# Four layers on one core: own instruction orders for the last slots of the token blocks

## The chip, the cores and the metric

The kernel runs on one core of one Trainium2 chip. The metric is the device time of one execution in microseconds (us), lower is better.

## What is computed

Sixteen sequences of 256 tokens of width 128 go through four layers, each followed by a residual and a layer norm:

```python
x = layernorm(x + mamba(x))            # layer a: state space block
x = layernorm(x + expert_attention(x)) # layer b: 8 heads of 64, 8 experts
x = layernorm(x + linear_attention(x)) # layer c: 16 heads, rotary, gelu
x = layernorm(x + soft_experts(x))     # layer d: softmax over batches and over slots
```

In layer b each token and head picks one of 8 value experts and one of 8 output experts by the largest gate; `values = x @ value_expert[sel]`, causal attention, then the sum over heads of `out @ output_expert[sel]`. Layer c computes q and k with gelu, rotates them, builds one k^T v per head, and normalises. A layer norm needs `1 / sqrt(variance + eps)` of each token.

## The kernel before

`token_blocks` does layers a, b and c, one batch (a sequence of 256 tokens, two halves c = 0, 1 of 128) at a time; `soft_experts` does layer d for all batches and can begin only when the last batch's rows are in DRAM (`x3_stored`), since its softmax goes over the batches.

The token blocks are a software pipeline, written out by hand. Each engine has a function `slot(r, u, a, b, o, c, more)`, which issues in a fixed order the steps of four batches: in slot t layer a of batch t, the attention of layer b of batch t-1, its expert mixing (called o) of batch t-2, layer c of batch t-3. At the end the flags a, b, o switch off: slot 16 has attention of batch 15, mixing of 14, layer c of 13; slot 17 has mixing of 15 and layer c of 14; slot 18 has layer c of 15 alone. Batch 14 is called Y and batch 15 Z. Every engine works its queue in order; semaphores say when a step of another engine is done. The order of the steps in `slot` therefore decides who waits.

Steps of layer b, attention: `b_values(b,u,e)` on TensorE multiplies by value expert e; `b_v(b,e)` on VectorE (L1267) keeps the rows that chose it; `b_scores(b,hp)` computes two heads' scores, `b_max` (L1278) their maxima, `b_probs` on ScalarE the exponentials, `b_turn` transposes them, `b_pt` copies them back, `b_pv` multiplies with the values, `b_rgb` spreads the scale factors, `b_ot` (L1297) applies them. The scores, the transposed scores and the even experts' values share one pair of banks, `ps_v[0]`.

Mixing: `b_choice(b,u,c)` spreads each token's choice into bank `ps_m`; `b_mo(b,u,c,e)` on VectorE (L1308) makes the masked operand, a product, in one of MO = 4 buffers; `b_out(b,c,e)` on TensorE (L630) multiplies it with output expert e and adds into `ps_u`, a part of bank pair `ps_v[1]`. There are 16 of each for a batch. `b_start` puts the residual into `ps_u` first and waits until all values of the next batch are selected, because the odd experts' values go through the same bank. `b_oa` copies the sum, `b_oat` (L639) transposes it into `ps_o`, `b_res` and `b_x2` (L333) normalise it, `b_x2t` (L645) transposes it back.

Layer c: `c_qk`, `c_v`, `c_rot`, `c_krt`, `c_kv`, `c_out` on TensorE all use bank `ps_c`, one after another; `c_q`, `c_v`, `c_qr`, `c_kv`, `c_res`, `c_ln`, `c_x3` (L1381) are VectorE's part; `c_x3t` transposes the result and copies it to be stored. The store of a batch (L368, L372) reads the single buffers `x3` and `x3T`, so `c_x3(b)` waits until both stores of every earlier batch have landed (32 of `x3_stored` for each).

The reciprocal root of a norm is `newton` (L59), run by GpSimd on tiles of 128 x 2: 15 small operations, 14 of them each dependent on one before.

```python
def wait(eng, sem, value):
    if not isinstance(value, int) or value > 0:
        eng.wait_ge(sem, value)
```

Of the kernel before, what the change touches and what calls it, by code (L numbers as in the profile page):

```python
# [2309 lines left out]
```

## Time and profile before

| | |
|---|---|
| median of 3 runs | 1631.72 us (1630.33 to 1632.02) |
| the profiled execution | 1630.81 us, span of its instructions 1628.9 us |
| TensorE matmul busy | 1472.9 us, 90% of the span |
| VectorE busy | 1239.2 us, 76% |
| ScalarE, GpSimd busy | 799.8 us and 791.1 us, 49% each |
| mean granted TensorE clock | 0.97 of 2.4 GHz |

Slots 16 to 18 lie between 988 and 1119 us of the span. Busy time is what the profile sees an engine execute; a matmul's end is modelled, so two matmuls in a row overlap in the listing, and the time from start to start is what one costs. A time in square brackets is how long the engine was idle before that row, with the instruction that ended it.

### The profile page before, as it was taken

What the parts mean: (1) busy time and instruction counts of PE and PEld (TensorE: products, weight loads), DVE (VectorE), ACT (ScalarE), POOL (GpSimd) and SP (SyncE); (2) the same over time, 40 slices, a digit from 0 to 9 for tenths busy, and PEclk for the clock granted to TensorE, in tenths of its full rate; (3) what the DMA queues carried; (4) which work ended last, traced back from release to release, by engine and by line L of the source; (5) the groups of instructions that cost most, each with busy time, mean ns of one, the idle gap of its engine ahead of it and who ended that gap; (6) DMA issues with size and microseconds to landing.
All of it is one profiled execution on the core that took longest, in us unless ns stands there. A gap on an engine that the chain in (4) does not pass through costs nothing. (4 is left out here: it accounts for less than half of the span.)

```text
span 1628.9 us, 33875 instructions
## 1 busy us (share of the span) xinstructions
PE 1472.9 (90%) x11136; PEld 1275.7 (78%) x11136; DVE 1239.2 (76%) x2450; ACT 799.8 (49%) x1782; POOL 791.1 (49%) x2004
## 2 busy tenths in 40 slices
PE   5489999999999999999999999763899999869997
PEld 4366777778777878878778877653899999869997
DVE  4477798898898898898898887542888888836764
ACT  2144444444444544544544543301577677657775
POOL 0332253453453453453553462221777777647764
PEclk9998999999999999999999999875999999989999
DMA  6000000000000000000000000004876776877882
GB/s 228 7 7 1 8 1 14 15 1 14 15 1 14 14 1 14 14 1 14 14 1 14 8 1 8 7 7 133 208 191 184 201 199 177 243 256 299 315 315 75
DMA packets 140762, 132.20 MB, mean 81 GB/s; under 512 B 7377, under 2 KB 130513, under 8 KB 134097
## 3 DMA queue, kind: packets, MB, share of 16 engines
q1 hardware_dynamic: 140624, 130.50, 25.4%
q8 instruction: 71, 1.16, 0.3%
q14 instruction: 67, 0.54, 0.1%
HBM read 73.85 MB, written 56.62 MB: 80 GB/s over the span
## 5 line engine op out<-in xcount | busy, mean ns | idle before, releaser
L630 PE MATMUL bk<-ve_f,oe 128*128 128x128 f32 x2048 | 277.3, 281 | 3.3 <-DVE ve_f L1308 3.3
L630 PEld LDWEIGHTS bk<-ve_f,oe 128*128 128x128 f32 x2048 | 249.4, 193 | 29.4 <-issue 21.9
L1308 DVE SCALAR_TENSOR_TENSOR ve_f<-ps_m,oT 128x512 f32<-128x512 f32 x256 | 172.5, 682 | 5.6 <-PE bk L630 3.5
L2198 POOL TENSOR_TENSOR d_s<-d_ex 128x1024 f32<-128x1024 f32 x32 | 131.8, 4118 | 86.4 <-ACT d_ex L1998 86.4
L1267 DVE COPY_PREDICATED vals<-oh,bk 128x512 f32<-128x512 int32 x224 | 150.5, 725 | 10.1 <-PE bk L398 9.4
L1948 PE MATMUL d_sl<-d_ex,e_prT 128*128 128x128 f32 x1024 | 136.2, 277 | 8.9 <-POOL d_ex L2215 8.9
L1882 PE MATMUL d_lg<-d_phf,d_xtf 128*128 (+1 forms) x1024 | 125.7, 283 | 14.4 <-DMA d_xtf<-x_T 6.8
L1882 PEld LDWEIGHTS d_lg<-d_phf,d_xtf 128*128 128x128 f32 x1024 | 122.7, 200 | 15.2 <-issue 7.2
L1948 PEld LDWEIGHTS d_sl<-d_ex,e_prT 128*128 128x128 f32 x1024 | 125.5, 194 | 9.1 <-POOL d_ex L2215 9.1
L1892 PE MATMUL d_sl<-d_ex,d_xs 128*128 128x128 f32 x1024 | 121.4, 277 | 5.1 <-DVE d_ex L2113 5.1
L977 ACT ACTIVATE ve_f<-bk,r 128x128 f32<-128x128 f32 x128 | 47.3, 370 | 158.5 <-DVE r L1281 158.3
L396 PE MATMUL bk<-veH,x1H 128*128 128x512 f32 x256 | 116.3, 454 | 7.3 <-DVE vals L1267 7.2
L1892 PEld LDWEIGHTS d_sl<-d_ex,d_xs 128*128 128x128 f32 x1024 | 118.5, 194 | 5.5 <-DVE d_ex L2113 5.5
L2095 DVE TENSOR_REDUCE d_nm<-d_lg 128x128 f32<-128x2048 f32 x32 | 73.3, 2291 | 48.2 <-PE d_lg L1882 46.1
L63 POOL TENSOR_SCALAR lnB_v<-lnB_mv 128x2 f32<-128x2 f32 x16 | 3.1, 192 | 213.6 <-DVE lnB_mv L322 213.6
L879 ACT ACTIVATE pt<-bk 128x384 f32<-128x384 f32 x128 | 61.7, 499 | 90.2 <-PE bk L568 89.1
L398 PE MATMUL bk<-veH,x1L 128*128 128x512 f32 x256 | 101.1, 395 | 0.0
L397 PE MATMUL bk<-veL,x1H 128*128 128x512 f32 x256 | 101.1, 395 | 0.0
L2050 ACT ACTIVATE e_prT<-d_lg 128x512 f32<-128x512 f32 x128 | 72.5, 595 | 47.6 <-PE d_lg L1935 47.5
L2215 POOL TENSOR_TENSOR d_ex<-d_ex,e_bias 128x1024 f32<-128x1024 f32 x32 | 74.8, 2366 | 40.0 <-DMA d_ex<-y_slots 39.9
L1142 DVE SCALAR_TENSOR_TENSOR cacc<-cin,cw,cacc 128x256 f32<-128x256 f32 x192 | 86.6, 495 | 3.0 <-ACT cin L879 3.0
L1993 ACT ACTIVATE d_raw<-d_lg 128x512 f32<-128x512 f32 x128 | 71.5, 601 | 32.4 <-PE d_lg L1882 16.5
(285 smaller groups left out, 3748.1 us busy)
## 6 DMA issues: line engine op xcount, KB each, us to landing
logits<-d_raw SPq DMA_DIRECT2D x128, 256.0 KB, 3.4
e_lt<-logits SPq DMA_DIRECT2D x32, 1024.0 KB, 5.9
y_slots<-d_ys SPq DMA_DIRECT2D x64, 256.0 KB, 4.2
d_ex<-y_slots SPq DMA_DIRECT2D x16, 1024.0 KB, 7.6
d_w<-W SPq DMA_DIRECT2D x16, 256.0 KB, 3.4
oe<-xT SPq DMA_DIRECT2D x1, 2048.0 KB, 7.9
xt_in<-xT SPq DMA_DIRECT2D x16, 128.0 KB, 2.3
x_in<-x SPq DMA_DIRECT2D x16, 128.0 KB, 2.4
```

The costliest lines, as they stand in the source:

```text
L396: pe.matmul(ps, lh, rh, start=first, stop=False, skip_group_check=True)
L397: pe.matmul(ps, lh, rl, start=False, stop=False, skip_group_check=True)
L398: return pe.matmul(ps, ll, rh, start=False, stop=last, skip_group_check=True)
L630: last = pe.matmul(ps_u[:, cols], oe[:, hp, e, :], mo[:, n % MO, hp, :], start=False, stop=(e == NE - 1 and hp == HP - 1), skip_group_chec ...
L1142: V.scalar_tensor_tensor(cacc[:, ch, :], cin[:, ch, tap:tap + L], cw[:, ch, tap:tap + 1], cacc[:, ch, :], ALU.mult, ALU.add).then_inc(q["a ...
L1267: ins = V.copy_predicated(vals[:, c, :, :], oh[:, c, :, e:e + 1].bitcast(I32).to_broadcast([P, HB, DH]), ps_v[e % 2][:, c, :].rearrange("p ...
L1308: V.scalar_tensor_tensor(mo[:, n % MO, :, :].rearrange("p a n -> p (a n)"), ps_m[:], float(NE - e), oT[:, u, c, :, :].rearrange("p a n -> ...
L1882: last = pe.matmul(lg[:, k, i, :], xtf[:, b, c, :], phf[:, cols], start=(i == 0), stop=(i == BB - 1), skip_group_check=True)
L1892: last = pe.matmul(sl[:, k, i, :], xs[:, (BK * i + k) * C + c, :], ex[:, u, c, k, i, :], start=(c == 0 and i == 0), stop=(c == C - 1), ski ...
L1948: last = pe.matmul(po[:, c, :], prT[:, c, s, :], yb[:, v, s, :], start=(s == 0), stop=(s == SB - 1), skip_group_check=True)
L2198: G.tensor_tensor(s8[:], part[:, 0:8, :], part[:, 8:16, :], ALU.add).then_inc(n, 1)
L2215: G.tensor_tensor(yb[:, v, rows, :], yb[:, v, rows, :], bias[:, rows, :], ALU.add).then_inc(e["y"], 1)
```

## The change

Slots 16, 17 and 18 are no longer calls of `slot`; each engine has one written list of the steps of all three. `b_start(Y)` and the `b_out(Y)` now stand among the values of Z, `b_choice(Z,1,0)` and `b_oat(Y)` before the end of Z's attention, and layer c of Y among the `b_out(Z)`. Four helper functions choose the bank: the sum and the transposed rows of Y go to `ps_a` (layer a's, free by then), the second choice and layer c of Z to the two halves of `ps_v[0]`. The last batch's three roots (`lnB`, `lnC`, `lnD`) are issued on VectorE with the same `newton`. All other lines of the diff (some two hundred, of which one is shown) write `wait(eng, ...)` as `eng.wait_ge(...)` where the value is positive.

```diff
+Y, Z = NB - 2, NB - 1
+
+def sum_of(b):
+    return ps_a[:, 0:L] if b == Y else ps_u
+
+def rows_of(b):
+    return ps_a[:, L:2 * L] if b == Y else ps_o[:, L:2 * L]
+
+def chosen_of(b, c):
+    return bank[0][:, 1, :] if (b, c) == (Z, 1) else ps_m[:]
+
+def linear_of(b):
+    return bank[0][:, 0, :] if b == Z else ps_c
...
-        wait(sp, q["c_x3"], b + 1)
+        sp.wait_ge(q["c_x3"], b + 1)
...
+        if (b, c) != (Z, 1):
+            wait(pe, q["b_mo"], OUTS * b + NE * c)
+        else:
+            wait(pe, q["b_pt"], HB * NB)
...
     def b_start(b, u):
 
-        wait(pe, q["b_v"], (NE - 1) * capped(b + 2))
-        pe.matmul(ps_u, id_r[:], x1H[:, u, :], start=True, stop=False, skip_group_check=True)
-        pe.matmul(ps_u, id_r[:], x1L[:, u, :], start=False, stop=False,
+        if b == Y:
+            wait(pe, q["a_x1h"], NB)
+            wait(pe, q["a_x1l"], NB)
+        else:
+            wait(pe, q["b_v"], (NE - 1) * capped(b + 2))
+        pe.matmul(sum_of(b), id_r[:], x1H[:, u, :], start=True, stop=False, skip_group_check=True)
+        pe.matmul(sum_of(b), id_r[:], x1L[:, u, :], start=False, stop=False,
                   skip_group_check=True).then_inc(q["b_start"], 1)
...
     def b_oat(b):
-        wait(pe, q["b_oa"], b + 1)
-        wait(pe, q["b_ot"], HP * capped(b + 2))
-        wait(pe, q["b_eg"], capped(b + 3))
+        pe.wait_ge(q["b_oa"], b + 1)
+        if b != Y:
+            pe.wait_ge(q["b_ot"], HP * capped(b + 2))
+            pe.wait_ge(q["b_eg"], capped(b + 3))
         for c in range(C):
-            last = pe.transpose(ps_o[:, L + c * P:L + (c + 1) * P], oa[:, c * P:(c + 1) * P], id_f[:])
+            last = pe.transpose(rows_of(b)[:, c * P:(c + 1) * P], oa[:, c * P:(c + 1) * P], id_f[:])
         last.then_inc(q["b_oat_ps"], 1)
...
     def c_qk(b, u):
-        wait(pe, q["b_x2t"], b + 1)
-        wait(pe, q["c_x3t"], b)
+        pe.wait_ge(q["b_x2t"], b + 1)
+        if b == Z:
+            wait(pe, q["b_pt"], HB * NB)
+        else:
...
-    slot(NB // 2, 0, False, True, True, True, False)
-    slot(NB // 2, 1, False, False, True, True, False)
-    slot(NB // 2 + 1, 0, False, False, False, True, False)
+    b_choice(Y, 0, 0)
+    b_qk(Z, 1, 0)
+    b_gates(Z, 1)
+    b_oat(Y - 1)
+    b_qk(Z, 1, 1)
+    b_qk(Z, 1, 2)
+    b_qk(Z, 1, 3)
+    b_start(Y, 0)
+    b_values(Z, 1, 0)
+    b_out(Y, 0, 0)
+    b_values(Z, 1, 1)
+    b_out(Y, 0, 1)
+    b_values(Z, 1, 2)
+    b_values(Z, 1, 3)
+    b_x2t(Y - 1, 1)
+    b_out(Y, 0, 2)
+    b_values(Z, 1, 4)
+    b_values(Z, 1, 5)
+    c_qk(Y - 1, 1)
+    b_out(Y, 0, 3)
+    b_values(Z, 1, 6)
+    b_values(Z, 1, 7)
+    c_v(Y - 1, 1)
+    b_scores(Z, 0)
+    c_rot(Y - 1)
+    b_out(Y, 0, 4)
+    b_oht(Z)
+    c_krt(Y - 1)
+    b_out(Y, 0, 5)
+    c_kv(Y - 1)
+    b_turn(Z, 0)
+    c_out(Y - 1)
+    b_out(Y, 0, 6)
+    b_turn(Z, 1)
+    b_scores(Z, 1)
+    b_out(Y, 0, 7)
+    b_choice(Y, 0, 1)
+    b_rgb(Z, 0)
+    b_pv(Z, 0)
+    b_out(Y, 1, 0)
+    b_turn(Z, 2)
+    b_turn(Z, 3)
+    b_out(Y, 1, 1)
+    b_scores(Z, 2)
+    b_out(Y, 1, 2)
+    b_pv(Z, 1)
+    b_out(Y, 1, 3)
+    b_turn(Z, 4)
+    b_out(Y, 1, 4)
+    b_rgb(Z, 1)
+    b_turn(Z, 5)
+    b_out(Y, 1, 5)
+    b_scores(Z, 3)
+    b_out(Y, 1, 6)
+    b_pv(Z, 2)
+    b_rgb(Z, 2)
+    b_out(Y, 1, 7)
+    b_choice(Z, 1, 0)
+    c_x3t(Y - 1)
+    b_turn(Z, 6)
+    b_turn(Z, 7)
+    b_oat(Y)
+    b_rgb(Z, 3)
+    b_pv(Z, 3)
+    b_choice(Z, 1, 1)
+    b_start(Z, 1)
+    b_out(Z, 0, 0)
+    b_x2t(Y, 0)
+    b_out(Z, 0, 1)
+    b_out(Z, 0, 2)
+    c_qk(Y, 0)
+    b_out(Z, 0, 3)
+    b_out(Z, 0, 4)
+    c_v(Y, 0)
+    b_out(Z, 0, 5)
+    c_rot(Y)
+    b_out(Z, 0, 6)
+    b_out(Z, 0, 7)
+    c_krt(Y)
+    b_out(Z, 1, 0)
+    c_kv(Y)
+    b_out(Z, 1, 1)
+    b_out(Z, 1, 2)
+    c_out(Y)
+    b_out(Z, 1, 3)
+    b_out(Z, 1, 4)
+    b_out(Z, 1, 5)
+    b_out(Z, 1, 6)
+    b_out(Z, 1, 7)
+    b_oat(Z)
+    b_x2t(Z, 1)
+    c_qk(Z, 1)
+    c_v(Z, 1)
+    c_rot(Z)
+    c_krt(Z)
+    c_kv(Z)
+    c_out(Z)
+    c_x3t(Y)
+    c_x3t(Z)
...
+    b_eg(Z)
+    b_qk(Z, 0)
+    b_qk(Z, 1)
+    b_qk(Z, 2)
+    b_qk(Z, 3)
+    b_v0(Z)
+    b_x2t(Y - 1, 1)
+    c_gelu(Y - 1)
+    b_probs(Z, 0)
+    c_kr(Y - 1)
+    b_probs(Z, 1)
+    b_oht(Z, 1)
+    b_pt(Z, 0)
+    b_pt(Z, 1)
+    b_probs(Z, 2)
+    b_rgb(Z, 0)
+    b_probs(Z, 3)
+    b_pt(Z, 2)
+    b_pt(Z, 3)
+    b_probs(Z, 4)
+    b_probs(Z, 5)
+    b_pt(Z, 4)
+    b_pt(Z, 5)
+    b_rgb(Z, 1)
+    b_probs(Z, 6)
+    b_probs(Z, 7)
+    b_rgb(Z, 2)
+    c_x3t(Y - 1)
+    b_pt(Z, 6)
+    b_pt(Z, 7)
+    b_oa(Y)
+    b_rgb(Z, 3)
+    b_x2t(Y, 0)
+    c_gelu(Y)
+    c_kr(Y)
+    b_oa(Z)
+    b_x2t(Z, 1)
+    c_gelu(Z)
+    c_kr(Z)
+    c_x3t(Y)
+    c_x3t(Z)
...
+    b_gate(Z)
+    b_res(Y - 1)
+    b_mo(Y, 0, 0, 0)
+    b_mo(Y, 0, 0, 1)
+    b_v(Z, 1)
+    b_v(Z, 2)
+    b_x2(Y - 1, 1)
+    b_v(Z, 3)
+    b_mo(Y, 0, 0, 2)
+    b_v(Z, 4)
+    b_v(Z, 5)
+    b_mo(Y, 0, 0, 3)
+    b_v(Z, 6)
+    c_q(Y - 1)
+    b_v(Z, 7)
+    c_v(Y - 1)
+    b_max(Z, 0)
+    c_qr(Y - 1)
+    b_mo(Y, 0, 0, 4)
+    b_mo(Y, 0, 0, 5)
+    c_kv(Y - 1)
+    b_rg(Z, 0)
+    b_mo(Y, 0, 0, 6)
+    c_res(Y - 1, 1)
+    b_mo(Y, 0, 0, 7)
+    b_max(Z, 1)
+    b_mo(Y, 0, 1, 0)
+    b_mo(Y, 0, 1, 1)
+    b_ot(Z, 1, 0)
+    b_mo(Y, 0, 1, 2)
+    b_max(Z, 2)
+    b_rg(Z, 1)
+    c_ln(Y - 1)
+    b_mo(Y, 0, 1, 3)
+    b_mo(Y, 0, 1, 4)
+    b_ot(Z, 1, 1)
+    b_mo(Y, 0, 1, 5)
+    b_max(Z, 3)
+    b_rg(Z, 2)
+    b_mo(Y, 0, 1, 6)
+    c_x3(Y - 1)
+    b_mo(Y, 0, 1, 7)
+    b_ot(Z, 1, 2)
+    b_rg(Z, 3)
+    b_res(Y)
+    b_ot(Z, 1, 3)
+    b_mo(Z, 1, 0, 0)
+    b_x2(Y, 0)
+    b_mo(Z, 1, 0, 1)
+    b_mo(Z, 1, 0, 2)
+    b_mo(Z, 1, 0, 3)
+    b_mo(Z, 1, 0, 4)
+    c_q(Y)
+    c_v(Y)
+    b_mo(Z, 1, 0, 5)
+    b_mo(Z, 1, 0, 6)
+    c_qr(Y)
+    b_mo(Z, 1, 0, 7)
+    b_mo(Z, 1, 1, 0)
+    c_kv(Y)
+    b_mo(Z, 1, 1, 1)
+    b_mo(Z, 1, 1, 2)
+    b_mo(Z, 1, 1, 3)
+    c_res(Y, 0)
+    b_mo(Z, 1, 1, 4)
+    b_mo(Z, 1, 1, 5)
+    b_mo(Z, 1, 1, 6)
+    b_mo(Z, 1, 1, 7)
+    b_res(Z)
+    rsqrt(dve, "lnB", Z, 1.0, EPS, norms["lnB"]["moments"], 2 * C)
+    b_x2(Z, 1)
+    c_ln(Y)
+    c_q(Z)
+    c_v(Z)
+    c_qr(Z)
+    c_kv(Z)
+    c_res(Z, 1)
+    rsqrt(dve, "lnC", Z, 1.0, 1e-12, norms["lnC"]["moments"], 2 * C)
+    c_x3(Y)
+    c_ln(Z)
+    rsqrt(dve, "lnD", Z, 1.0, EPS, norms["lnD"]["moments"], 2 * C)
+    c_x3(Z)
...
+    rsqrt(pool, "lnB", Y - 1, 1.0, EPS, norms["lnB"]["moments"], 2 * C)
+    c_km(Y - 1)
+    c_turn(Y - 1)
+    b_vg(Z)
+    rsqrt(pool, "lnC", Y - 1, 1.0, 1e-12, norms["lnC"]["moments"], 2 * C)
+    rsqrt(pool, "lnD", Y - 1, 1.0, EPS, norms["lnD"]["moments"], 2 * C)
+    rsqrt(pool, "lnB", Y, 1.0, EPS, norms["lnB"]["moments"], 2 * C)
+    c_km(Y)
+    c_turn(Y)
+    rsqrt(pool, "lnC", Y, 1.0, 1e-12, norms["lnC"]["moments"], 2 * C)
+    rsqrt(pool, "lnD", Y, 1.0, EPS, norms["lnD"]["moments"], 2 * C)
+    c_km(Z)
+    c_turn(Z)
```

The lists shown are TensorE's, ScalarE's, VectorE's and GpSimd's, in this order; each takes the place of the same three calls of `slot`.

## Rows read from the trace of the kernel before

**Rows 1.** Stretches A, B, C and the hand-over: start:end, length, busy, clock, DMA.

```profile
987.99:1042.15 54.16, 50.48 (x379) 40.68 (x378) 37.80 (x87) 20.66 (x60) 12.84 (x50) 1.00 0.02 6
1042.15:1083.32 41.17, 26.52 (x168) 22.29 (x169) 19.50 (x47) 3.80 (x9) 10.94 (x48) 0.83 0.02 7
1083.32:1118.24 34.92, 10.27 (x28) 6.09 (x28) 8.71 (x29) 1.92 (x6) 10.93 (x48) 0.53 0.01 4
1118.24:1126.37 8.13, 0.69 (x3) 0.32 (x3) 0.60 (x2) 0.38 (x1) 0.00 (x0) 0.50 0.38 115
```

**Rows 2.** TensorE's timeline in A: start, length, line, tiles, idle before.

```profile
992.79 0.40 PE L396 MATMUL bk<-veH,x1H 128*128 128x512 f32 x1
...
994.19 0.39 PE L396 MATMUL bk<-veH,x1H 128*128 128x512 f32 x1
...
1009.99 1.10 PE L668 MATMUL ps_c<-ql,rot_s 128*128 128x512 f32 x2
1010.92 1.05 PE L630 MATMUL bk<-ve_f,oe 128*128 128x128 f32 x8
1011.81 0.27 PE L540 MATMUL ps_o<-id_f,oh 128*128 128x128 f32 x1
...
1024.29 0.38 PE L552 MATMUL bk<-negb,id_b 128*128 128x256 bf16 x2
...
1025.45 1.16 PE L630 MATMUL bk<-ve_f,oe 128*128 128x128 f32 x8
1026.54 0.65 PE L582 MATMUL ps_o<-pt,vals 128*64 128x256 f32 x4
```

**Rows 3.** VectorE's timeline in A.

```profile
999.41 1.33 DVE L1267 COPY_PREDICATED vals<-oh,bk 128x512 f32<-128x512 int32 x2
1000.63 0.68 DVE L1308 SCALAR_TENSOR_TENSOR ve_f<-ps_m,oT 128x512 f32<-128x512 f32 x1
...
1015.24 0.17 DVE L1289 RECIPROCAL rg<-rs 128x4 f32<-128x4 f32 x1
1015.44 0.17 DVE L1291 TENSOR_TENSOR rg<-rg,gx 128x4 f32<-128x4 f32 x1
...
1025.57 0.96 DVE L1278 TENSOR_REDUCE r<-bk 128x6 f32<-128x768 f32 x1 [0.39 <-PE bk L560]
...
1029.17 0.66 DVE L1308 SCALAR_TENSOR_TENSOR ve_f<-ps_m,oT 128x512 f32<-128x512 f32 x1
```

**Rows 4.** TensorE's timeline in B.

```profile
1043.19 0.41 PE L639 MATMUL ps_o<-id_f,oa 128*128 128x128 f32 x2 [0.71 <-issue]
1049.84 0.69 PE L645 MATMUL ps_o<-id_f,x 128*128 128x128 f32 x2 [6.24 <-DVE x L333]
...
1057.76 1.13 PE L630 MATMUL bk<-ve_f,oe 128*128 128x128 f32 x8
...
1078.05 1.80 PE L630 MATMUL bk<-ve_f,oe 128*128 128x128 f32 x8 [2.32 <-DVE ve_f L1308]
...
1080.08 2.77 PE L630 MATMUL bk<-ve_f,oe 128*128 128x128 f32 x16
```

**Rows 5.** TensorE on tile ps_c, a batch earlier: start:end, length, busy, clock.

```profile
948.00:961.00 13.00, 4.78 (x24) 1.00 0.00 1
```

**Rows 6.** VectorE's timeline in B and C.

```profile
1062.89 0.19 DVE L1352 TENSOR_SCALAR zd<-ps_c 128x32 f32<-128x32 f32 x1 [1.16 <-PE ps_c L690]
...
1065.42 1.28 DVE L1308 SCALAR_TENSOR_TENSOR ve_f<-ps_m,oT 128x512 f32<-128x512 f32 x2
...
1089.22 0.73 DVE L333 TENSOR_SCALAR x<-ps_o,lnB_mv,lnB_y 128x128 f32<-128x128 f32 x2 [4.63 <-POOL lnB_y L76]
...
1111.28 0.60 DVE L333 TENSOR_SCALAR ncn<-rc,lnC_mv,lnC_y 128x128 f32<-128x128 f32 x2 [4.33 <-POOL lnC_y L76]
...
1118.24 0.60 DVE L1381 TENSOR_SCALAR x<-n,lnD_mv,lnD_y 128x128 f32<-128x128 f32 x2 [4.64 <-POOL lnD_y L76]
```

**Rows 7.** Waits of the DMA queue at the end of C: total, times, longest.

```profile
SPq L106 <- DMA x_T<-x3T: 1.4, 1, 1.4
```

More of the change, by code:

```diff
@@ L370, in store @@
                 sp.wait_ge(x_all_in, 32)
-                wait(sp, q["c_x3t"], b + 1)
+                sp.wait_ge(q["c_x3t"], b + 1)
                 sp.dma_start(x3T_dram[:, bass.ds(b * L, L)], x3T[:]).then_inc(x3_stored, 16)
@@ L627, in b_out @@
                 cols = slice(c * P, (c + 1) * P)
-                wait(pe, q["b_mo"], OUTS * b + n + 1)
+                pe.wait_ge(q["b_mo"], OUTS * b + n + 1)
                 for hp in range(HP):
-                    last = pe.matmul(ps_u[:, cols], oe[:, hp, e, :], mo[:, n % MO, hp, :], start=False,
+                    last = pe.matmul(sum_of(b)[:, cols], oe[:, hp, e, :], mo[:, n % MO, hp, :], start=False,
                                      stop=(e == NE - 1 and hp == HP - 1), skip_group_check=True)
@@ L694, in c_x3t @@
             def c_x3t(b):
-                wait(pe, q["c_x3"], b + 1)
+                pe.wait_ge(q["c_x3"], b + 1)
                 for c in range(C):
-                    last = pe.transpose(ps_c[:, c * P:(c + 1) * P], x3[:, c, :], id_f[:])
+                    last = pe.transpose(linear_of(b)[:, c * P:(c + 1) * P], x3[:, c, :], id_f[:])
                 last.then_inc(q["c_x3t_ps"], 1)
@@ L882, in a_cin @@
             def a_cin(b, half):
-                wait(act, q["a_xbc_ps"], 2 * b + half + 1)
+                act.wait_ge(q["a_xbc_ps"], 2 * b + half + 1)
                 wait(act, q["a_conv"], NCH * (TAPS - 1) * b)
@@ L970, in b_probs @@
                 hp, s, a = h // 2, h // 2 % 2, h % 2
-                wait(act, q["b_max"], 2 * HP * b + 2 * hp + 2)
+                act.wait_ge(q["b_max"], 2 * HP * b + 2 * hp + 2)
                 if h >= 4:
@@ L1132, in a_conv @@
             def a_conv(b, half, taps=range(1, TAPS)):
-                wait(dve, q["a_cin"], 2 * b + half + 1)
+                dve.wait_ge(q["a_cin"], 2 * b + half + 1)
                 n0 = (TAPS - 1) * (NCH * b + 2 * half)
@@ L1293, in b_ot @@
             def b_ot(b, u, hp):
-                wait(dve, q["b_rgb"], HP * b + hp + 1)
+                dve.wait_ge(q["b_rgb"], HP * b + hp + 1)
                 wait(dve, q["b_mo"], OUTS * (b - 1))
@@ L1611, in b_vg @@
             def b_vg(b):
-                wait(pool, q["b_v"], (NE - 1) * (b + 1))
+                pool.wait_ge(q["b_v"], (NE - 1) * (b + 1))
                 for c in range(C):
@@ L1625, in c_turn @@
             def c_turn(b):
-                wait(pool, q["c_q"], b + 1)
+                pool.wait_ge(q["c_q"], b + 1)
                 wait(pool, q["c_qr"], 2 * b)
@@ L1802, in store @@
                 sp.wait_ge(ready, READY)
-                wait(sp, e["rows"], C * (b + 1))
+                sp.wait_ge(e["rows"], C * (b + 1))
                 sp.dma_start(out[bass.ds(b * L, L), :].rearrange("(c p) d -> p c d", p=P), xo[:, u, :, :]
```

329 lines of the change are left out of this document (160 added, 169 removed).

## The prediction

> **What bounds the kernel now.** I read the stretches first [rows 1]. The work around the change is three stretches at the end of the token blocks. In the first (987.99 to 1042.15 us, call it A: experts' mixing of batch Y, attention of batch Z) TensorE is busy 50.5 of 54.2 us at full clock, so it sets the pace. In the second (to 1083.32, B: mixing of Z, linear attention of Y) it is busy 26.5 of 41.2 us. In the third (to 1118.24, C: linear attention of Z alone) 10.3 of 34.9 us: there nothing is loaded and one chain of dependent steps sets the time. The soft experts can't begin before the last store, and nothing in them changes, so what A, B and C gain or lose is what the program gains or loses. The timelines of TensorE and VectorE in these stretches [rows 2 to 6] say what each chain is made of.
>
> **What changes nothing.** Most of the diff's lines write the helper `wait` out as `wait_ge`. The helper only leaves out waits on zero or less; all those rewritten are positive. The instructions are the same, cost 0, wherever they stand. The banks of the last two batches take no instruction either; they only permit orders.
>
> **A, the cost.** Work first: the instructions are those of before plus `b_choice(Z,1,0)` and `b_oat(Y)`, together 0.6 us of TensorE. Then waits. Before, TensorE stood idle 3.7 us of A [rows 1]. VectorE had made up to four products `b_mo` before TensorE wanted the first, because `b_start` and all `b_out` stood behind the values and the first scores. In the new order each `b_out(Y,c,e)` stands on TensorE almost directly behind the place where VectorE makes its product, and TensorE takes its queue in order, so whatever VectorE does first is waited for by the values and scores queued behind. I walk both queues with these units: one expert's values 1.40 us, one `b_out` 0.89 to 1.09, one `b_scores` 1.16, the rotation 0.93 [rows 2]; one `b_v` 1.22, one `b_mo` 0.68 when awaited, and from the start of a `b_max` through `b_rg` and `c_ln` to the end of the next product 4.26 [rows 3]; 0.1 to 0.2 from TensorE's last issue to a reader, 0.05 back.
> - `b_out(Y,0,2)` stands before `b_values(Z,4)`; its product stands behind `b_v` 2, `b_x2` and `b_v` 3. `b_v` 2 can start when values 2 are there, 6.2 us into the values (three blocks of values, two of products), so the product is ready 3.8 us later; from 0.2 before until then TensorE has only values 3 and a transpose to do, 1.6: it waits 2.4.
> - `b_out(Y,0,3)` stands before values 6, its product behind `b_v` 5: 1.5.
> - `b_out(Y,0,4)` stands behind the rotation, its product behind `c_qr`, two 512-wide operations like the product itself: 0.2 + 1.4 + 0.7, and 0.3 to 0.7 for `b_max` before them: 2.9.
> - `b_out(Y,1,3)`: product behind `b_max(Z,2)`, `b_rg`, `c_ln`: 0.2 + 4.3, with a `b_out` and a `b_pv` (1.7) to do meanwhile: 2.9.
> - `b_out(Y,1,5)`: product behind `b_ot(1)`, which needs `b_rgb(1)` on ScalarE, queued behind `b_pt` 5: 2.2.
> - `b_out(Y,1,6)` directly behind `b_scores(Z,3)`: product behind `b_max(3)`, `b_rg`: 2.3.
> - `b_oat(Y)` waits for ScalarE's last `b_pt` and `b_oa`: 1.4. Nine small ones (gates, turns, rotation, `c_out`) 2.6.
>
> That is 18.2; each wait is seen about 0.12 shorter because the modelled end of a matmul covers its start, 1.9 over the sixteen, so 16.3 against 3.7. A grows by 12.6 + 0.6, of which I take 12.9 since the long `b_max` is uncertain. Bounds: 0.6 if TensorE never waits more than before, and 15 if each small wait doubles.
>
> **B, the gain.** Before, `b_oat(Y)` starts 1.0 after A and `b_x2t(Y)` 6.65 later; the first `b_out` of Z comes only at 1057.76, behind three linear steps of Y at half clock [rows 4]. New: `b_oat(Y)` is in A, 1.5 before its end, so `b_x2t(Y)` stands 5.1 after A's end; VectorE waits in `b_x2(Y)` for GpSimd's root with the products of Z queued behind, so only `b_out(Z,0,0)` is done by then. From `b_x2t` on: 15 `b_out` at 0.93 are 14.0, six linear steps 3.7 (their rows come to 4.8 with the modelled ends, some 0.17 each [rows 5]), `b_x2t` 0.2. Waits: first product 0.4, `b_out(Z,0,5)` behind `c_v` 1.3, `b_out(Z,0,7)` behind `c_qr` 1.4, `b_out(Z,1,1)` behind `c_kv` 1.1, `b_out(Z,1,4)` behind `c_res` (2.5 from its first operation to the next product [rows 6]) 2.6, `b_oa` 0.6: 7.4. So B is 5.1 + 25.3 = 30.4 against 41.2: minus 10.8. Bounds: minus 18 without these waits, minus 7 if they come to half as much again.
>
> **C, the gain.** VectorE waits three times for GpSimd's roots: 4.63, 4.33, 4.64 us [rows 6]. The root has 15 operations, of which 14 hang on each other. VectorE's own small dependent operations start 0.20 apart, 0.17 long [rows 3]: 14 of them 2.8, and 0.2 for the two that don't wait and for handing over: 3.0. No row shows a root on VectorE; below, 14 at 0.16 are 2.3, above, GpSimd's 4.6 with nothing gained. I take 3.0, nearest to the same operations on the same engine. Gain 1.6 for the first. For the second 1.3 less (`xc`, hidden before by the wait, is now ahead of the root, 0.35), and `c_x3(Y)` (0.5) stands before `c_ln(Z)`: 0.8. For the third 1.6. Sum minus 4.0, bounds 0.5 more and minus 6. `c_ln(Y)` (2.2) is put between `b_x2(Z)` and `c_q(Z)`, where VectorE waits 4.3 for TensorE and ScalarE: hidden; without that cover it would cost 2.2. A wait is added: `c_x3(Z)` needs both stores of Y, and these are now late, because TensorE's `c_x3t(Y)` stands behind `c_out(Z)`. From `c_x3(Y)` to the landed store: transposes 0.7, copy 0.4, handovers 0.2, and some 1.9 to landing (the queue waited 1.4 for the last such store after issuing it [rows 7]): 3.2. `c_ln(Z)` and its root take 2.2 + 3.0: 2.0 to spare, cost 0.
>
> The Trainium skill ("VectorE: DVE Perf Modes", section on the TRN2 errata) gives a fixed cost of about 150 cycles at 0.96 GHz for each VectorE operation, by which a root would be some 2.4 us, an estimate, and C would gain 1.8 more; the trace's 0.20 between starts is what I use.
>
> **The clock.** After 2.3 us of idle at 1078 the granted clock fell from 2.4 to 1.2 GHz: eight matmuls of a `b_out` took 1.80 us, the next sixteen 2.77 [rows 4], against 0.89 and 1.8: with a transpose about 2.0 lost. A now has five waits of 2.2 to 2.9. Where TensorE is slow before a wait that VectorE sets, the wait swallows part of it. I take a third of one such spell, plus 0.7; bounds 0 and four spells, plus 8.
>
> **Sum.** 12.9 - 10.8 - 4.0 + 0.7 = -1.2. The profiled execution took 1630.81 us (span 1628.9 and 1.9 around it), 0.9 under the median, which is inside the runs' spread, so the difference is applied to the median: 1631.7 - 1.2 = 1630.5. Of the full gain of B some nine tenths is paid in A.
>
> **Rivals.**
> 1. Products in time. If VectorE is ahead of the walk in A (the `b_out` set among the values fill holes that VectorE left TensorE there), then half of A's 12.9 is gone: -7.7, 1624.0; with all of it gone 1617.6. For it: TensorE has only 51 us of work in A. Against it: the queues are in order, and behind `b_scores(Z,3)` and `b_scores(Z,2)` there is nothing else to take. It decides when A stays under 65 us.
> 2. The clock falls in A, slower than before. Four waits over 2 us, each followed by 2.0 lost: -1.9 + 8.0 = +6.1, 1637.8. For it: the fall at 1078 after 2.3 us. Against it: that one came after shorter waits, and before it TensorE, with idle times between the products, had kept the full clock from 1058 on; the 0.83 of B [rows 1] is mostly the 11 us after the wait of 6.24. It decides from three spells on (+4). The Trainium skill ("TensorE: Matmul & The Clock Gate", section on HAM oscillation) says that gaps in a matmul stream bring the clock down again and again, each burst starting slow; by it the change would cost, not gain.
> 3. The roots do not profit: 15 operations on VectorE take GpSimd's 4.6, or the store of Y holds `c_x3(Z)`. C gains nothing and loses 0.85: 1630.5 + 4.8 = 1635.3.
>
> **How the numbers follow.** No measurement of this kernel can tell 0.2% (3.3 us) from no change. Forecast 0.42, its own range 1627 to 1634, a tenth of it over the bound of faster; rival 1 0.31; rival 2 0.20; rival 3 0.07. Faster: 0.31 and 0.04, 0.35. Slower: 0.20 and 0.05 of rival 3, 0.25. Same: 0.40. From three quarters of rival 1 to all of rival 2: 1621 to 1638.
>
> **What would show it.** In the changed profile: A between the first `b_choice(Y,0,0)` and the last `b_pv(Z)` near 67 us, with waits of TensorE on the products (line of `b_mo`) near 14 us in sum; `b_oat(Y)` before the last `b_pv`; B near 30; in C no GpSimd root, 15 small operations of VectorE in 3.0 us, three times; granted clock 1.0 over most of A. The sum is wrong if A is under 65 us, if the clock in A is under 0.9, or if VectorE waits before the last `c_x3` on a DMA.

## The result: 0.6% slower

The changed kernel takes 1641.70 us (median of 8 runs, 1638.78 to 1643.76) against 1631.74 us before, measured alongside (8 runs, 1629.91 to 1636.39): ratio 1.0059, 95% interval 1.0046 to 1.0071. The forecast was 1630.5 in a range of 1621 to 1638; the time is outside it, 3.9 us beyond the time of rival 2.

The three stretches of the changed kernel, cut at the same steps as those of before [rows 1]. The columns are start:end, length, busy time of TensorE, its weight loads, VectorE, ScalarE and GpSimd, TensorE's granted clock, DMA share, GB/s:

```profile
988.84:1063.25 74.41, 59.27 (x384) 47.78 (x382) 38.62 (x91) 20.73 (x60) 13.09 (x51) 0.89 0.02 6
1063.25:1095.05 31.80, 22.44 (x162) 20.17 (x161) 15.80 (x33) 3.75 (x8) 7.79 (x32) 0.95 0.00 1
1095.05:1126.34 31.29, 10.95 (x30) 6.37 (x30) 18.24 (x84) 2.08 (x6) 4.84 (x18) 0.57 0.03 9
```

| | before | predicted | after |
|---|---|---|---|
| A | 54.2 | 67.1, with the clock 67.8 | 74.4 |
| B | 41.2 | 30.4 | 31.8 |
| C | 34.9 | 30.9 | 31.3 |
| sum | 130.3 | 129.1 | 137.5 |

A to C account for 7.2 of the 10.0 us between the medians. The profiled span grew by 10.7 us: A begins 0.85 later, and from the first matmul of the soft experts to the end it takes 505.0 us instead of 502.5. That code is the same. Over the sixteen profiles of this document this last part varied from 502.4 to 507.5 and the start of A from 984.8 to 991.1, and kernels that differ only in A to C lie anywhere in these ranges. The records of the granted clock account for the spread of the last part: TensorE ran 31.5 us of it at 1.2 GHz before, 37.4 us after and 43.2 us in the profile with 507.5, and its length less half of that slow time is 485.7 to 487.2 us in all sixteen. So the stages are compared in the profiles, the whole by medians and intervals, and a difference of a few us in one profile's span says nothing about an edit.

Every term but one came out near its forecast. The one is the clock. This is TensorE in A in steps of 4 us, from the windows view (PE busy, granted clock, DMA share, GB/s); in the windows of A not shown it was 0.87 to 1.00:

```profile
1005.00:1009.00 4.00, 4.00 (x17) 0.70 0.00 0
...
1021.00:1025.00 4.00, 3.59 (x19) 0.57 0.00 0
...
1041.00:1045.00 4.00, 3.63 (x18) 0.57 0.00 0
...
1049.00:1053.00 4.00, 3.17 (x17) 0.65 0.01 4
1053.00:1057.00 4.00, 2.67 (x18) 0.77 0.11 33
1057.00:1061.00 4.00, 3.73 (x30) 0.80 0.00 0
```

Before, A ran at 1.00 throughout [rows 1]. The waits that the walk had listed are there. The waits view of A says how much TensorE waited for the products (in all, times, longest):

```profile
PE ps_a L651 <- DVE ve_f L1467: 11.9, 7, 2.6
```

and TensorE's timeline shows what follows them (L651 is `b_out`, L410 to L412 the values, L554 and L699 transposes):

```profile
1004.15 2.08 PE L651 MATMUL ps_a<-ve_f,oe 128*128 128x128 f32 x8 [1.37 <-DVE ve_f L1467]
1005.88 0.77 PE L410 MATMUL bk<-veH,x1H 128*128 128x512 f32 x1
1006.45 0.63 PE L411 MATMUL bk<-veL,x1H 128*128 128x512 f32 x1
...
1011.74 1.16 PE L651 MATMUL ps_a<-ve_f,oe 128*128 128x128 f32 x8 [1.27 <-DVE ve_f L1467]
1012.66 0.48 PE L410 MATMUL bk<-veH,x1H 128*128 128x512 f32 x1
...
1021.41 2.08 PE L651 MATMUL ps_a<-ve_f,oe 128*128 128x128 f32 x8 [2.57 <-DVE ve_f L1467]
1023.28 0.42 PE L554 MATMUL ps_o<-id_f,oh 128*128 128x128 f32 x1
```

The eight records of a `b_out` (four f32 matmuls, each listed as two) take 1.16 us at 2.4 GHz and 2.08 at 1.2 GHz, and a record of the values 0.39 and up to 0.77. After a wait of 1.37 us they ran slow, after one of 1.27 they did not, after 2.57 slow again. The length of one wait is not all that differed: ahead of the 1.37 stood two transposes and a wait of 0.70, ahead of the 1.27 more than 6 us of matmuls without a gap. The values of Z that stand behind the product are slow too, and VectorE needs them for its next selection. This is how long VectorE waited for the values behind the first slow product, in the changed kernel and, at the same step, in the kernel of experiment 3 that keeps the clock at 1.00:

```profile
1008.30 2.81 DVE L1426 COPY_PREDICATED vals<-oh,bk 128x512 f32<-128x512 int32 x4 [4.21 <-PE bk L412]
```

```profile
1006.14 2.82 DVE L1436 COPY_PREDICATED vals<-oh,bk 128x512 f32<-128x512 int32 x4 [2.71 <-PE bk L412]
```

4.21 us against 2.71: the slow matmuls are on the path in A, and the next wait does not swallow them.

VectorE at the first of these waits shows the coupling (L1426 selects the values, L347 is the norm, L1467 the product):

```profile
1000.33 1.34 DVE L1426 COPY_PREDICATED vals<-oh,bk 128x512 f32<-128x512 int32 x2 [0.95 <-PE bk L412]
1001.57 0.71 DVE L347 TENSOR_SCALAR x<-ps_o,lnB_mv,lnB_y 128x128 f32<-128x128 f32 x2
1002.20 1.32 DVE L1426 COPY_PREDICATED vals<-oh,bk 128x512 f32<-128x512 int32 x2
1003.43 0.67 DVE L1467 SCALAR_TENSOR_TENSOR ve_f<-ps_m,oT 128x512 f32<-128x512 f32 x1
```

The product of `b_out(Y,0,2)` is the fourth thing that VectorE does after TensorE released it at 1000.33, and TensorE had two things left to do: the queue of each engine waits for the other in turn.

C has the roots on VectorE. The third one, with the first of the operations before it on the same numbers and the store's input behind it:

```profile
1122.73 0.37 DVE L336 BATCH_NORM_AGGREGATE lnD_mv<-lnD_st 128x2 f32<-128x6 f32 x2
1123.20 0.17 DVE L63 TENSOR_SCALAR lnD_v<-lnD_mv 128x2 f32<-128x2 f32 x1
1123.48 0.17 DVE L65 TENSOR_SCALAR lnD_h<-lnD_v 128x2 f32<-128x2 f32 x1
1123.56 0.16 DVE L66 TENSOR_SCALAR lnD_y<-lnD_v 128x2 int32<-128x2 int32 x1
1123.75 0.16 DVE L70 TENSOR_TENSOR lnD_t<-lnD_y 128x2 f32<-128x2 f32 x1
...
1126.14 0.16 DVE L76 TENSOR_TENSOR lnD_y<-lnD_y,lnD_t 128x2 f32<-128x2 f32 x1
1126.34 0.60 DVE L1540 TENSOR_SCALAR x<-n,lnD_mv,lnD_y 128x128 f32<-128x128 f32 x2
```

From the aggregate's end to `c_x3` it took 3.2 us, where GpSimd's root kept VectorE waiting 4.64 [rows 6]. There is no wait for a store in front of `c_x3`.

### The profile page after: what moved, and what is told of

Its sections match the earlier page's. It is cut to its first block and busy times, and to the rows that moved or that the text cites. A ratio compares the mean times of both kernels' runs of the same rounds, so it can differ in the third digit from the quotient of the medians.

```text
span 1639.6 us, 33875 instructions
## 1 busy us (share of the span) xinstructions
PE 1480.1 (90%) x11136; PEld 1284.0 (78%) x11136; DVE 1244.7 (76%) x2495; ACT 800.1 (49%) x1782; POOL 785.9 (48%) x1959
## 3 DMA queue, kind: packets, MB, share of 16 engines
q8 instruction: 71, 1.16, 0.3%
## 5 line engine op out<-in xcount | busy, mean ns | idle before, releaser
L651 PE MATMUL bk<-ve_f,oe 128*128 128x128 f32 x1920 | 261.2, 281 | 7.0 <-DVE ve_f L1467 6.8
L651 PEld LDWEIGHTS bk<-ve_f,oe 128*128 128x128 f32 x1920 | 234.1, 193 | 32.1 <-issue 22.7
L1467 DVE SCALAR_TENSOR_TENSOR ve_f<-ps_m,oT 128x512 f32<-128x512 f32 x248 | 166.8, 680 | 1.7 <-PE bk L651 0.8
L1426 DVE COPY_PREDICATED vals<-oh,bk 128x512 f32<-128x512 int32 x224 | 150.3, 723 | 18.7 <-PE bk L412 17.9
L410 PE MATMUL bk<-veH,x1H 128*128 128x512 f32 x256 | 116.5, 455 | 6.3 <-DVE vals L1426 6.3
L412 PE MATMUL bk<-veH,x1L 128*128 128x512 f32 x256 | 101.4, 396 | 0.0
L2241 ACT ACTIVATE d_raw<-d_lg 128x512 f32<-128x512 f32 x128 | 71.6, 602 | 35.1 <-PE d_lg L2130 17.9
```

What stands on the lines that cost most here:

```text
L410: pe.matmul(ps, lh, rh, start=first, stop=False, skip_group_check=True)
L412: return pe.matmul(ps, ll, rh, start=False, stop=last, skip_group_check=True)
L651: last = pe.matmul(sum_of(b)[:, cols], oe[:, hp, e, :], mo[:, n % MO, hp, :], start=False, stop=(e == NE - 1 and hp == HP - 1), skip_group ...
L1426: ins = V.copy_predicated(vals[:, c, :, :], oh[:, c, :, e:e + 1].bitcast(I32).to_broadcast([P, HB, DH]), ps_v[e % 2][:, c, :].rearrange("p ...
L1467: V.scalar_tensor_tensor(mo[:, n % MO, :, :].rearrange("p a n -> p (a n)"), chosen_of(b, c), float(NE - e), oT[:, u, c, :, :].rearrange("p ...
```

## The experiments

Fourteen further kernels were measured, in five sets; "before" was measured anew in each set, and ratios are against it. A, B and C come from one profile of each kernel. "Idle matmuls" are matmuls whose result nobody reads.

| kernel | us | ratio to before (95%) | A | B | C |
|---|---|---|---|---|---|
| before | 1631.7 | | 54.2 | 41.2 | 34.9 |
| after | 1641.7 | 1.0059 (1.0046, 1.0071) | 74.4 | 31.8 | 31.3 |
| A as before | 1623.9 | 0.9960 (0.9943, 0.9976) | 54.2 | 34.2 | 31.3 |
| same, four products of Z ahead | 1621.2 | 0.9936 (0.9918, 0.9954) | 54.1 | 34.1 | 31.3 |
| product two places earlier than its `b_out` | 1622.5 | 0.9944 (0.9927, 0.9962) | 54.6 | 33.2 | 31.3 |
| one place | 1624.0 | 0.9933 (0.9919, 0.9946) | 56.4 | 33.2 | 31.3 |
| changed, 74 idle matmuls in A | 1638.1 | 1.0045 (1.0028, 1.0062) | 70.2 | 34.3 | 31.3 |
| changed, 45 idle matmuls in A | 1635.2 | 1.0014 (1.0003, 1.0024) | 66.8 | 34.7 | 31.3 |
| changed, roots on GpSimd | 1645.9 | 1.0064 (1.0050, 1.0077) | 75.0 | 31.9 | 35.1 |
| before, roots on VectorE | 1628.8 | 0.9963 (0.9951, 0.9976) | A + B 95.3 | | 30.8 |
| two places, late residual | 1620.0 | 0.9914 (0.9899, 0.9928) | 54.6 | 30.4 | 31.3 |
| same, 55 idle matmuls in C | 1618.8 | 0.9902 (0.9887, 0.9917) | 54.6 | 30.1 | 30.4 |
| same, 69 in B and C | 1614.5 | 0.9884 (0.9868, 0.9900) | 54.6 | 28.1 | 30.4 |
| same, 40 in B and C | 1618.2 | 0.9910 (0.9895, 0.9924) | 54.6 | 27.6 | 31.0 |
| same, 71 more at the end | 1621.2 | 0.9920 (0.9902, 0.9937) | 54.6 | 27.7 | 31.0 |
| 42, GpSimd's order mended | 1614.0 | 0.9893 (0.9877, 0.9910) | 54.6 | 27.6 | 29.2 |

The median of "before" was 1631.6, 1635.3, 1633.7, 1633.3 and 1631.4 us in the five sets, so lines of different sets are compared by ratio.

**1. Is the loss in A alone?** Slot 16 as it was, everything behind it new; then the same with `b_x2(Y)` and `b_x2t(Y)` behind four products and three `b_out` of Z.

```diff
 # TensorE; the other engines in the same way
-b_choice(Y, 0, 0)
...
-b_out(Y, 1, 7)
+slot(NB // 2, 0, False, True, True, True, False)
+b_oat(Y)
 b_choice(Z, 1, 0)
-c_x3t(Y - 1)
...
-b_pv(Z, 3)
 b_choice(Z, 1, 1)
 b_start(Z, 1)
```

> Slot 16 is issued as before the change (the old function slot on all four engines); the written orders, the banks and the roots on VectorE are kept from the end of A on, with b_oat(Y) and b_choice(Z,1,0) first on TensorE. Theory 1 (the loss is all made in A, by waits of TensorE on products and by the lower clock they bring): A is 54 us again, B about 32 (6.7 to b_x2t(Y) and 25 from there), C 31.3 as in the changed kernel, so 54 + 33 + 31 = 118 to 119 against 130.3 of before: 11 to 12 us under the kernel before, near 1620. Theory 2 (the new orders of B and C lose too, or the last stage is slowed by something the change brings): not under 1628.

> As old_a, and in B VectorE makes the products 0 to 3 of Z and TensorE multiplies 0 to 2 before the norm of Y (b_x2, b_x2t stand behind them), inside the 4.4 us that GpSimd's root takes. Theory 1: two more b_out lie in that wait, 1.5 to 2 us under old_a, near 1618. Theory 2: the wait was not empty, no difference to old_a.

With the old A the rest of the change is a gain of 0.4%: 1623.9 us, 7.7 under "before" where 11 to 12 were expected; the stretches of its profile sum to 10.6 less. C keeps the 3.6 us it had won, B 7.0 of its 9.4. The first outputs ahead of the norm saved the wait before `b_x2t(Y)` (1.80 instead of 3.56 us), yet B stayed at 34.1: `c_qk(Y)` then waited for the copy, at half clock. The ratios' intervals overlap, so nothing is shown for that order.

**2. Are the waits the distance between a product and its use?** Only TensorE's list is changed: each `b_out(Y)` stands where the next one (or the second next) stood; VectorE's list stays. The edit for two:

```diff
 b_values(Z, 1, 0)
-b_out(Y, 0, 0)
 b_values(Z, 1, 1)
-b_out(Y, 0, 1)
 b_values(Z, 1, 2)
 b_values(Z, 1, 3)
 b_x2t(Y - 1, 1)
-b_out(Y, 0, 2)
+b_out(Y, 0, 0)
...
+b_out(Y, 1, 5)
+b_out(Y, 1, 6)
 b_out(Y, 1, 7)
```

> The changed kernel, with only the places of b_out(Y) on TensorE in A moved: b_out number n stands where number n+2 stood, the last three stand together. VectorE's order is untouched. Theory 1: products are two ahead, so the waits of TensorE on them in A (some 12 us seen) go below 4, the clock stays up, and A falls from 74.4 to about 60 us; total near 1627. Theory 2 (VectorE's chain in A is the limit, whatever TensorE does): A stays above 68, total above 1635.

> The changed kernel with each product's matmuls of batch Y placed one product later on TensorE (two later gave A 54.6 us and 1622.5). Coupling theory (TensorE waits because each product is asked for 1.7 to 2 us after the VectorE work that precedes it has been released by TensorE itself; one product of distance removes most of it, and waits under 1.3 us bring no fall of the clock): A 56 to 60 us, clock 1.00 over A, about 1625 us. Rival (the waits are a shortage of VectorE time over the whole of A, so that a shift only moves them): A 65 us or more, 1632 us or more.

Two places: the same steps, the same instructions, and A falls from 74.4 to 54.6 us. TensorE's `b_out` in A from the view of groups (busy, mean ns, idle before), and the stretch:

```profile
L651 PE MATMUL ps_a<-ve_f,oe 128*128 128x128 f32 x128 | 17.3, 280 | 0.0
```

```profile
990.22:1044.83 54.61, 50.54 (x384) 41.10 (x383) 38.77 (x91) 20.62 (x60) 13.09 (x51) 1.00 0.03 8
```

The 11.9 us of waits are gone and the clock is 1.00. One place leaves 1.2 us of waits, no slow window, A 56.4. So VectorE had time enough over the whole of A, and one place of distance covers all but 1.2 us of the lateness. The rival (a shortage of VectorE) is out.

**3. How much of A is the clock?** The changed kernel, with idle matmuls (an identity times itself, into a region that the transposes overwrite later; the output is not touched) in front of the `b_out` that wait. First 74 of them, then, as each turned out to take 0.23 us (the profile lists each as two records), 45, sized to the six waits.

```diff
+def fill(n):
+    for _ in range(n):
+        pe.matmul(ps_a[:, L:L + P], id_f[:], id_f[:], start=False, stop=False, skip_group_check=True)
...
 b_x2t(Y - 1, 1)
+fill(5)                 # 8 in the first version
 b_out(Y, 0, 2)
```

> The changed kernel with idle matmuls of 128 x 128 (74 of them, into the unused half of Y's bank, whose content is overwritten later) in front of the six b_out(Y) in A that wait longest, 8 to 16 each, always shorter than the wait. They do no work of the computation. Theory 1, with the clock as the mis-sized term: the granted clock stays at 2.4 GHz in A, A falls from 74.4 to about 67.5, total 6 to 7 us under the changed kernel, near 1635. Theory 3 (the slow stretches lie in the shadow of waits and cost nothing): no gain, 1641 or, where the filler is late, more.

> The changed kernel with 45 idle 128x128 matmuls (0.23 us each) in front of the six waits of A, sized to the waits of the changed kernel (1.37, 1.27, 2.57, 2.47, 1.91 and 2.15 us: 5, 5, 10, 10, 7 and 8 of them) in place of the 74 of before, which ended up to 1.3 us late. Clock theory (all of A's 7.0 us over the prediction is the clock): the granted clock stays at 1.00 and A falls from 74.4 to about 67.5 us, about 1635 us. Rival (only 4.2 us are the clock, the rest are waits that the walk had too short): A stays at 70 us, about 1638 us.

With 45 the stretch A and its groups are:

```profile
988.16:1054.95 66.79, 62.04 (x475) 51.69 (x474) 38.65 (x91) 20.70 (x60) 13.01 (x51) 1.00 0.02 7
```

```profile
L651 PE MATMUL ps_a<-ve_f,oe 128*128 128x128 f32 x128 | 18.1, 284 | 1.5 <-DVE ve_f L1477 1.5
L657 PE MATMUL ps_a<-id_f 128*128 128x128 f32 x90 | 11.2, 277 | 0.0
```

The real work, the orders and the places of the waits are the same; TensorE is only kept from standing idle. The clock is 1.00 and A is 66.8 instead of 74.4 us: the half clock costs 7.6 us of A, and what is left, 66.8, is close to the 67.1 of the walk. The loss is no accident of one profile: the kernel of experiment 4 with the roots on GpSimd has the same A, and there the clock fell again, after waits of 1.38, 2.58, 2.47 and 1.91 us, and A took 75.0 us. The first version shows the price of too many: clock 1.00 as well, but idle matmuls that ended after the product was ready (3.73 us of them before a wait of 2.57) kept A at 70.2. The whole went from a ratio of 1.0059 to one of 1.0014, 0.45% or 7.3 us.

B, 31.8 us in the changed kernel, was 34.7 here though nothing in it differs. The last 32 matmuls of `b_out(Z)`, behind the same wait of 2.32 us, in the changed kernel and in this one:

```profile
1090.74 3.84 PE L651 MATMUL bk<-ve_f,oe 128*128 128x128 f32 x32 [2.32 <-DVE ve_f L1467]
```

```profile
1082.43 6.76 PE L651 MATMUL bk<-ve_f,oe 128*128 128x128 f32 x32 [2.32 <-DVE ve_f L1477]
```

The same wait was followed by 3.84 us (also with A as before and with the roots on GpSimd), by 5.18, 5.20, 5.30 and 5.47 in four other kernels, and by 6.76 here. Where it was 3.84 the clock did not fall. A wait of this length is no certain loss: over these eight kernels it cost 0 to 2.9 us, and what decides between them is not shown.

**4. What are the roots worth?** Roots of Z back on GpSimd in the changed kernel; and the kernel before with nothing but the three roots on VectorE.

```diff
 b_res(Z)
-rsqrt(dve, "lnB", Z, 1.0, EPS, norms["lnB"]["moments"], 2 * C)   # lnC and lnD too
 b_x2(Z, 1)
```

> The changed kernel with the three roots of the last batch back on GpSimd, everything else kept. Theory (the roots on VectorE are worth 3.6 us, and the whole loss lies in A): C grows from 31.3 back to about 35, A and B stay at 74 and 32, so about 1645.5 us, ratio to before about 1.0085. Rival (the roots on VectorE cost something elsewhere, or were already hidden, and belong to the loss): the time stays at 1641 to 1642.

> The kernel before with one edit: the three roots of the last batch run on VectorE. Theory: only C changes, 34.9 us becomes 31.3, A stays at 54.2 and B at 41.2, so about 1628 us, ratio 0.9978. Rival (the roots need the other parts of the change, such as the order of the last slot, to pay): within 0.1% of before.

C in the first and in the second kernel:

```profile
1095.18:1130.26 35.08, 10.95 (x30) 6.38 (x30) 11.34 (x38) 2.08 (x6) 13.93 (x63) 0.53 0.02 8
```

```profile
1083.78:1114.61 30.83, 10.26 (x28) 6.08 (x28) 15.69 (x74) 1.91 (x6) 1.93 (x3) 0.55 0.01 5
```

3.8 us by taking them away, 4.1 by adding them alone; alone they make the kernel 0.4% faster (0.9963, above the 0.2% expected, the interval ends at 0.9951 and 0.9976). For the first the expected ratio, 1.0085, did not come: its median lies 4.2 us above that of the changed kernel, but "before" stood 3.6 us higher in that set too, and the ratios 1.0064 and 1.0059 can't be told apart. The stretch shows the roots' worth there, the ratio doesn't.

**5. The residual of Y in B.** In B VectorE's `c_res(Y)` stood ahead of the last four products of Z, and TensorE had the wait of 2.32 us above. On top of the two places of experiment 2, it is moved into C, where VectorE waits; `c_ln(Y)`, in C already, goes three steps further back, and on GpSimd the root for it goes to the end:

```diff
-c_res(Y, 0)
 b_mo(Z, 1, 1, 4)
...
 b_x2(Z, 1)
-c_ln(Y)
+c_res(Y, 0)
 c_q(Z)
 c_v(Z)
 c_qr(Z)
+c_ln(Y)
```

> The kernel with the matmuls of batch Y two products later, and the residual and norms of the linear attention of Y (2.5 us of VectorE, and its root) moved out of B, behind the second norm of Z, where VectorE waits for TensorE. Theory (the last four products of Z wait in B for these 2.5 us, 2.3 of them as a wait of TensorE): B 33.3 becomes about 31, C stays at 31.3 to 32, about 1620 us, ratio 0.993. Rival (C has no room for it: the same 2.5 us come back there, or the roots of Y on GpSimd end too late for the last store): 1622 us or more, as without the edit.

B 30.4 instead of 33.2, C the same 31.3: 2.8 us. The wait of 2.3 is gone, and so are the slow matmuls behind it: 32 records in 5.20 us with two places alone, 40 in 4.71 here, some 1.4 us less for the same 32. About 1 us of this went back to a longer spell at half clock earlier in B, behind the wait before `b_x2t(Y)`.

**6. The clock in B and C.** C ran at 0.53 before and at 0.57 after. Idle matmuls again, on the kernel of experiment 5, in banks that are free by then: 55 in C alone, then 69 in B and C (the counts shown), then 40 of them (the counts behind), then 71 more around the last two `c_x3t` and ahead of the first scores.

```diff
+fill(14)     # none in the first kernel, 8 in the version with 40
 b_x2t(Y, 0)
...
+fill(36)     # 19
 b_x2t(Z, 1)
 c_qk(Z, 1)
+fill(5)      # 4
 c_v(Z, 1)
+fill(3)      # 2
 c_rot(Z)
+fill(9)      # 6
 c_krt(Z)
+fill(2)      # 1
 c_kv(Z)
```

> As the kernel with two products of distance and the late residual, plus idle 128x128 matmuls on TensorE (55 in all, results never read) in front of the operations of the last linear attention that wait for a norm, a copy or a rotation (36 of them before the transposes of the second norm). In that stretch the granted clock was 0.50 from 4 us after the last expert products to its end. Clock theory (TensorE's waits let the clock fall, and the chain then pays double for its matmuls: c_qk 2.07, c_v 1.22, rotation 2.04, transposes 0.69 and 0.69, sums 1.22, outputs about 1.9): at full clock these cost about half, so C falls from 31.3 to about 27 and the whole to about 1616 us. Rival (the half clock is not set by TensorE's own idleness, or the first waits hide the longer matmuls): C stays at 31 to 31.5 and the time at 1620, or it grows by fillers that end late.

> As the one above with 14 more idle matmuls before the transposes of the norm of Y, where TensorE waited 2.08 us and then ran 6 us at half clock (16 product matmuls 3.78 instead of 2.05, c_qk 1.91 instead of about 1.0). Clock theory: that spell goes and B falls from 30.4 to about 28, about 1614 us. Rival (VectorE sets the pace of B, with 16 products and the norms, and TensorE has slack in it): B stays within 0.5 us of 30.4 though the clock shows 1.00, and the time equals the one above.

> The kernel with two products of distance, the late residual and idle matmuls in B and C, now 40 of 0.23 us sized to the waits (8 before the norm of Y, 19 before the norm of Z, 4, 2, 6 and 1 behind it) in place of the 69 of before, which ended 1.2 us and 2.3 us after the norms. Clock theory: clock 1.00, B 28.4 becomes about 27.5, C 30.4 becomes about 27, about 1610 us. Rival (the clock falls again in what is left of the waits, or the matmuls' length was hidden): C stays at 30 to 31, 1614 us or more.

> As the one above with 71 more idle matmuls: 24 and 20 before the transposes of the last two x3, 27 behind them, where TensorE waits 6.8 us for the first scores of the soft experts. Clock theory: the transposes take 0.38 instead of 0.69 us, the first 32 matmuls of the scores 3.5 instead of 5.3 us, together some 1 to 2 us less, about 1608.5 us. Rival (the scores' pace is set elsewhere, by the load of x_T or VectorE's exponentials): the same time as the one above, within 1 us.

In B it worked at once: clock 1.00, 28.1 and 27.6 us against 30.4. In C I had given each idle matmul 0.12 us where it takes 0.23, so 36 of them ended some 3 us after the norm (1081.3 against 1078.2) and C won 0.9 only. Sized right it was 31.0, no gain, for another reason. TensorE before the transposes of q and k, and GpSimd, whose 512-wide product for the rotation (L1877) VectorE needs first:

```profile
1085.40 0.44 PE L703 MATMUL bk<-id_f,qr 128*128 128x128 f32 x2 [2.88 <-DVE qr L1512]
```

```profile
1082.35 0.20 POOL L76 TENSOR_TENSOR lnC_y<-lnC_y,lnC_t 128x2 f32<-128x2 f32 x1
1082.63 0.19 POOL L1883 TENSOR_SCALAR km<-ks 128x1 f32<-128x1 f32 x1
1082.99 0.34 POOL L1885 TENSOR_SCALAR kmh<-h,km 128x16 f32<-128x16 f32 x1 [0.17 <-POOL km L1883]
1083.30 1.26 POOL L1877 TENSOR_TENSOR wq_f<-ql,cos_s 128x512 f32<-128x512 f32 x1
```

`ql` had been ready at about 1079.2; GpSimd was making Y's root, which experiment 5 had made late by moving `c_res(Y)`. With C slower this had been hidden. At the end, the 71 more idle matmuls gained nothing: from the last `c_x3` to the first scores it took 11.5 us instead of 8.1, as each group of transposes stood behind idle matmuls that ended late, and the first 32 matmuls of the scores took 6.22 us (6.00 without). The expected 3.5 did not come. Over the whole program the intervals of these four kernels overlap with that of experiment 5 (0.9899 to 0.9928), so what is shown of the gain in B is the stretch.

**7. GpSimd's order mended.** With it, 2 idle matmuls more ahead of the outputs.

```diff
 # GpSimd
 c_turn(Y)
-rsqrt(pool, "lnC", Y, ...)
 c_km(Z)
 c_turn(Z)
+rsqrt(pool, "lnC", Y, ...)
 # VectorE
 c_qr(Z)
-c_ln(Y)
 c_kv(Z)
+c_ln(Y)
```

> The kernel with two products of distance, the late residual and the sized idle matmuls, with one order mended: on GpSimd the product for the rotation of Z stands before the root of the third norm of Y, and VectorE's part that needs this root stands behind the product with the mask (2 idle matmuls more before the outputs). Theory (the 2.88 us wait before the transposes of the rotated q and k was GpSimd's queue): the wait falls to under 0.5 us, C falls from 31.0 to about 27.5 us, B stays at 28.0, the sum of A, B and C is about 110 us against 130.3 of before, 1611 to 1614 us. Rival (the root now ends too late, and the second root of Y with it): C stays at 30 us or more, 1615 us or more.

```profile
987.97:1042.53 54.56, 50.52 (x383) 41.05 (x381) 38.75 (x91) 20.59 (x60) 13.00 (x51) 1.00 0.03 8
1042.53:1070.17 27.64, 22.40 (x178) 20.32 (x176) 13.42 (x24) 3.74 (x8) 4.74 (x18) 1.00 0.00 1
1070.17:1099.38 29.21, 14.25 (x98) 11.88 (x98) 20.62 (x93) 2.08 (x6) 8.61 (x33) 0.81 0.03 10
```

The wait before these transposes is 0.17 us, C 29.2: 1.8 of the 3.5 expected. From the start of C the transposes come 2.7 us and the outputs 3.1 us earlier than in the version with 40, but `c_ln(Y)` now stands directly ahead of `c_res(Z)` on VectorE, which begins 2.3 us after the last output instead of at once. The stretches sum to 111.4 us against 130.3 of before; 1614.0 us, 1.1% faster than before. The version with 69 idle matmuls (0.9884) can't be told from it.

## Why the prediction was wrong

- **The step that failed is the clock**: "I take a third of one such spell, plus 0.7". It was 7.6 us in A alone, ten times that and close to the top bound of four spells (8), and with the fall in B, 1.6 us, it was beyond that bound. The argument for the third was that a wait set by VectorE swallows slow matmuls in front of it. In A what runs slow is also the values that VectorE selects next (it waited 4.21 us for them instead of 2.71), so the products behind them come later too.
- The same paragraph weighed the one row of a fall, 2.3 us of idle at 1078 [rows 4], as an exception because TensorE had stood partly idle before it. In the changed kernel the clock fell five times in A, after waits of 1.37 to 2.57 us, most of them with TensorE busy between them. Rival 2 named this mechanism and its point of decision; what came is rival 2 with six falls of some 1.5 us each instead of four of 2.0. It had a chance of 0.20, and the range ended at its time. The prediction's own sign, a clock under 0.9 in A, came too (0.89). The Trainium skill ("TensorE: Matmul & The Clock Gate", section on HAM oscillation) gave the direction rightly. But it describes longer waits than those of A; here 1.37 to 2.57 us were enough.
- **A's waits were right.** The walk gave 67.1 us without the clock; with the clock held at 1.00 it measured 66.8. The waits on the products were put at 14 us and came to 11.9 in seven waits, so the agreement of the sum to 0.3 us is better than that of its terms. That they are a matter of distance and not of VectorE's time is shown by experiment 2.
- **B**: 31.8 for 30.4. The sixteen records of `b_out` behind `b_x2t(Y)` took 3.62 us instead of 2.05, so the error is the clock again; without that fall and with the same waits B would be near 30.2, an estimate from these two numbers.
- **C**: minus 3.6 for minus 4.0. A root takes 3.2 us, not 3.0: the small operations start 0.20 apart as taken from [rows 3], but four of them, whose wait is an instruction of its own (`wait_apart`), start 0.26 to 0.28 after the one before. The estimate of 2.4 us for a root from the figure in the Trainium skill ("VectorE: DVE Perf Modes", section on the TRN2 errata) was lower than the 3.2 measured. The store of Y did not hold `c_x3(Z)`.
- Rival 1 (products in time) failed: A was not under 65 us. Rival 3 failed by experiment 4.
- That no measurement of this kernel can tell 0.2% from no change was too pessimistic: the intervals here are some 0.1 to 0.2% to either side, and 1.0014 (1.0003 to 1.0024) is already clear of 1.
- The rest of the difference, 10.0 us by medians against 7.2 in A to C, lies in code that is the same. In the profiles the last part is 2.5 us longer and has 5.9 us more at half clock, which would cost 2.95, so this is the clock as well. Why it fell for longer there, and whether the shift in time has a part in it, stays open.

## What to carry to other kernels

Interleave two engines' in-order queues with a distance: an operand made by one engine and used by the other one place later at the earliest, even if the sum of work says that there is room. Here one place of distance was worth 18 us of A, 7.6 of them the clock's, and cost no instruction.

When an edit turns one long idle time of TensorE into several of 1.4 us and more, price each as a possible fall of the clock, and ask whether what runs slow behind it feeds the engine that is waited for. Idle matmuls are a good test of this: where they end before the wait does, they change the clock and little else. They can be a gain where the waits can't go (experiment 3, 0.45%), and they lose where they end late.

When a part gets faster, look at what had been hidden behind it on a third engine before the gain is counted.
